# Starting the state-space layer of the first tile at once, and spreading the feed-forward weight quantisation over the first three passes

## Time and profile before

| | |
|---|---|
| median of three runs | 1433.84 us (1433.72 to 1434.61) |
| the profiled execution, its own time | 1433.73 us |
| its span, first to last instruction | 1431.3 us |
| instructions | 31673 |
| busy: PE, PE weight loads, DVE, ACT, POOL | 88%, 73%, 73%, 53%, 58% |
| mean granted TensorE clock | 0.98 |
| read and written in HBM | 19.74 MB, 4.19 MB |

### The profile page before, as it was taken

One profiled execution on the slowest core, in us unless ns is written; L12 is line 12 of the kernel. 1 busy time (PEld: TensorE's weight loads), 2 busy tenths in 40 slices (PEclk: granted clock), 3 DMA queues, 4 the chain that ended last, 5 costly groups with the idle time before them and its releaser, 6 DMA issues.

```text
span 1431.3 us, 31673 instructions
## 1 busy us (share of the span) xinstructions
PE 1266.4 (88%) x10486; PEld 1048.0 (73%) x10486; DVE 1043.3 (73%) x2485; ACT 755.8 (53%) x1740; POOL 827.7 (58%) x1404
## 2 busy tenths in 40 slices
PE   1478999999999999999999999999999999999874
PEld 0367887777787877777888777777887777878752
DVE  4546687777777777777877777778777777878655
ACT  1335455565555555655555556555555665555542
POOL 1425566565666665656666666566665666666541
PEclk9979999999999999999999999999999999999997
DMA  9100000000000000000000000000000000000000
GB/s 293 36 9 8 9 13 8 5 11 11 11 11 11 11 7 4 11 11 11 11 11 11 4 7 11 11 11 11 11 11 0 11 11 11 11 11 8 5 5 8
DMA packets 25361, 24.36 MB, mean 17 GB/s; under 512 B 6768, under 2 KB 23664, under 8 KB 25072
## 3 DMA queue, kind: packets, MB, share of 16 engines
q1 hardware_dynamic: 20848, 16.08, 3.7%
q10 hardware_dynamic: 4480, 7.86, 1.6%
HBM read 19.74 MB, written 4.19 MB: 17 GB/s over the span
## 4 chain that ended last, share of the span: by engine, by line
PE 47%; DVE 22%; POOL 14%; issue 9%; ACT 5%; SPq 1%; DMA 1%; DVEq 1%; POOLq 0%; ACTq 0%
PE bank L1344 15%; DVE xc L850 7%; POOL pr L440 5%; POOL pr L450 5%; PE bank L1336 5%; PE bank L1215 5%; PE bank L1149 3%; PE bank L1151 3%; PE bank L1150 3%; PE bank L1271 2%; PE bank L1166 2%; DVE h L997 2%; ACT h L683 2%; DVE h L1001 2%; PE bank L1324 2%
## 5 line engine op out<-in xcount | busy, mean ns | idle before, releaser
L1259 PE MATMUL bank<-xcT,wq 128*128 128x128 f32 x2048 | 238.5, 278 | 2.2 <-ACT xcT L629 2.2
L1259 PEld LDWEIGHTS bank<-xcT,wq 128*128 128x128 f32 x2048 | 233.3, 193 | 7.2 <-issue 2.0
L1344 PE MATMUL bank<-wo,oT 128*128 128x256 f32 x1024 | 231.3, 379 | 0.0
L1344 PEld LDWEIGHTS bank<-wo,oT 128*128 128x128 f32 x1024 | 191.8, 190 | 25.9
L850 DVE SCALAR_TENSOR_TENSOR xc<-bank,cw,xc 128x124 f32<-128x124 f32 (+2 forms) x576 | 163.8, 340 | 14.1 <-ACT xc L587 6.8
L450 POOL TENSOR_TENSOR pr<-pr,mx 128x512 f32<-128x512 f32 x64 | 78.9, 1254 | 90.5 <-DVE mx L963 90.5
L644 ACT ACTIVATE qT<-bank,bqT 128x128 f32<-128x128 f32 x384 | 108.4, 364 | 28.8 <-PE bank L1259 28.8
L652 ACT ACTIVATE q<-qT 128x512 f32<-128x512 f32 x128 | 81.4, 636 | 38.6 <-DVE qT L937 34.6
L997 DVE SCALAR_TENSOR_TENSOR h<-h,bank 128x512 f32<-128x512 f32 x64 | 44.0, 687 | 79.0 <-ACT h L683 79.0
L428 POOL TENSOR_TENSOR rq<-rq,minus_half 128x16 f32<-128x16 f32 x32 | 93.3, 2914 | 4.6 <-DVE rq L944 4.6
L1336 PE MATMUL bank<-pT,vb 64*128 64x256 f32 x512 | 72.9, 405 | 9.5 <-ACT pT L664 9.5
(11 more groups left out here) (233 smaller groups left out, 3273.6 us busy)
## 6 DMA issues: line engine op xcount, KB each, us to landing
x_in<-in_x SPq DMA_DIRECT2D x32, 128.0 KB, 2.0
c_in<-in_ctx SPq DMA_DIRECT2D x32, 128.0 KB, 2.0
out<-x SPq DMA_DIRECT2D x32, 128.0 KB, 1.7
wq<-in_L_xattn_Wq ACTq DMA_DIRECT2D x1, 2048.0 KB, 11.5
wo<-in_L_xattn_Wo ACTq DMA_DIRECT2D x1, 2048.0 KB, 19.3
w_in<-in_L_attn_W_in SPq DMA_DIRECT2D x1, 1288.0 KB, 11.7
qT<-in_L_ffn_w_gate ACTq DMA_DIRECT2D x1, 1024.0 KB, 6.7
q<-in_L_ffn_w_up SPq DMA_DIRECT2D x1, 1024.0 KB, 8.7
```

The source lines that it names most:

```text
L1259: last = mm(x_Qbank[g][:, (n % 4) * P:(n % 4 + 1) * P], wq[:, c, n * HD:(n + 1) * HD], xcT[:, c, :], start=(c == 0), stop=(c == DC - 1))
L1344: last = mm(X1[:, 0:D], oT[:, n, :, :], wo[:, n, :], start=(n == 0), stop=(n == NH - 1))
```

## The change: what it does

1. SP no longer issues w_up, and issues W_in (semaphore `w_in_l`) and W_out (`w_out_l`) after the twelve small weights. ACT issues w_gate, w_up and w_down as its first three instructions, w_down now into `oT`.
2. After its part of pass 0 (`body(0)`, which holds the load of x for tile 1), SP issues Wk (now into `pT`), Wv (now into `h_sq`), Wq, the two bias rows and Wo, which ACT issued before.
3. Pass -1 waits on PE for W_in alone; ACT makes `wz_hi` and POOL `wz_lo` ahead of it. W_out times norm_w, `wout_hi` and `wout_lo` come between pass -1 and pass 0, and PE waits for them before pass 0. `wk_hi`, `wv_hi`, `wk_lo`, `wv_lo` come between pass 0 and pass 1, and PE waits for them before pass 1.
4. The quantisation is cut into `w_sum`, `w_scale` and `w_round` on DVE, `w_total` and `w_turn` on PE and `w_turned` on ACT. They stand at chosen places inside passes -1, 0 and 1; w_gate is turned between pass 0 and 1, w_up and w_down between pass 1 and 2. Before pass 2 PE and DVE wait for all six copies. The totals use bank F0 in place of X0.
5. POOL computes the three constants `f_c` before pass 2 rather than before pass -1.

```diff
-        wk = q2[:, 0, :, :].rearrange("p h s -> p (h s)").rearrange("p (c n) -> p c n", c=DC)
-        wv = q2[:, 1, :, :].rearrange("p h s -> p (h s)").rearrange("p (c n) -> p c n", c=DC)
+        wk = pT[:].rearrange("p j n -> p (j n)").rearrange("p (c n) -> p c n", c=DC)
...
+        wv = h_sq[:].rearrange("p (c n) -> p c n", c=DC)
+        w_stage = [qT[:].rearrange("p a h s -> p (a h s)"), q2[:].rearrange("p a h s -> p (a h s)"),
+                   oT[:].rearrange("p h a s -> p (h a s)")]
+        w_tern = [hl[:].bitcast(BF16), h[:].bitcast(BF16), hl[:].bitcast(BF16)]
...
-            sp.dma_start(q2[:].rearrange("p a h s -> p (a h s)").rearrange("p (j n) -> p j n", n=D),
-                         w_up.rearrange("(j p) n -> p j n", p=P)).then_inc(s["w_up_l"].sem, 16)
-            sp.dma_start(w_in[:], W_in.rearrange("(c p) n -> p c n", p=P)).then_inc(s["w_mixer"].sem, 16)
...
-            sp.dma_start(w_out, W_out.rearrange("(j p) n -> p j n", p=P)).then_inc(s["w_mixer"].sem, 16)
+            sp.dma_start(w_in[:], W_in.rearrange("(c p) n -> p c n", p=P)).then_inc(s["w_in_l"].sem, 16)
+            sp.dma_start(w_out, W_out.rearrange("(j p) n -> p j n", p=P)).then_inc(s["w_out_l"].sem, 16)
             sp.dma_start(c_in[:], ctx_t[0]).then_inc(s["c_loaded"].sem, 16)
...
-            for i in range(5):
+            body(0)
+            sp.dma_start(wk, Wk.rearrange("(c p) n -> p c n", p=P)).then_inc(s["w_kv"].sem, 16)
+            sp.dma_start(wv, Wv.rearrange("(c p) n -> p c n", p=P)).then_inc(s["w_kv"].sem, 16)
+            sp.dma_start(wq[:], Wq.rearrange("(c p) n -> p c n", p=P)).then_inc(s["w_attn"].sem, 16)
+            sp.dma_start(bk_r[:], row(bk, NKV * HD)).then_inc(s["w_attn"].sem, 16)
+            sp.dma_start(bv_r[:], row(bv, NKV * HD)).then_inc(s["w_attn"].sem, 16)
+            sp.dma_start(wo[:], Wo.rearrange("(h p) n -> p h n", p=P)).then_inc(s["w_attn"].sem, 16)
+            for i in range(1, 5):
...
-            pool.wait_ge(s["w_mixer"].sem, 16 * W_MIXER)
-            g.tensor_tensor(w_out, w_out, bcast(nw[:, :].unsqueeze(2), [P, XCH, D]),
-                            ALU.mult).then_inc(s["p_wout"].sem, 1)
-            pool.wait_ge(s["p_hi"].sem, 2)
-            g.tensor_tensor(wz_lo[:], w_in[:, :, 0:DI], wz_hi[:].bitcast(F32), ALU.subtract).then_inc(s["p_lo"].sem, 1)
-            pool.wait_ge(s["p_wout"].sem, 1)
-            g.tensor_tensor(wout_lo[:], w_out, wout_hi[:].bitcast(F32), ALU.subtract).then_inc(s["p_lo"].sem, 1)
             pool.wait_ge(s["p_exp"].sem, 1)
             g.tensor_scalar(a_neg[:], a_neg[:], -1.0, None, ALU.mult).then_inc(s["p_scaled"].sem, 1)
-            pool.wait_ge(s["p_wout"].sem, 1)
...
+            pool.wait_ge(s["p_hi"].sem, 1)
+            g.tensor_tensor(wz_lo[:], w_in[:, :, 0:DI], wz_hi[:].bitcast(F32), ALU.subtract).then_inc(s["p_lo"].sem, 1)
+            body(*tiles(-1))
+            pool.wait_ge(s["w_out_l"].sem, 16)
+            g.tensor_tensor(w_out, w_out, bcast(nw[:, :].unsqueeze(2), [P, XCH, D]),
+                            ALU.mult).then_inc(s["p_wout"].sem, 1)
+            pool.wait_ge(s["p_hi"].sem, 2)
+            pool.wait_ge(s["p_wout"].sem, 1)
+            g.tensor_tensor(wout_lo[:], w_out, wout_hi[:].bitcast(F32), ALU.subtract).then_inc(s["p_lo"].sem, 1)
+            body(*tiles(0))
+            pool.wait_ge(s["p_hi"].sem, 3)
+            g.tensor_tensor(wk_lo[:], wk, wk_hi[:].bitcast(F32), ALU.subtract).then_inc(s["p_lo"].sem, 1)
+            pool.wait_ge(s["p_hi"].sem, 4)
+            g.tensor_tensor(wv_lo[:], wv, wv_hi[:].bitcast(F32), ALU.subtract).then_inc(s["p_lo"].sem, 1)
+            body(*tiles(1))
             pool.wait_ge(s["q_step"].sem, 9)
             g.tensor_scalar(f_c[:, 0:1], wmean[:, 0:1], 0.5 / QMAX, None, ALU.mult).then_inc(s["c_consts"].sem, 1)
             g.tensor_scalar(f_c[:, 1:2], wmean[:, 1:2], 1.0 / QMAX, None, ALU.mult).then_inc(s["c_consts"].sem, 1)
             g.tensor_scalar(f_c[:, 2:3], wmean[:, 2:3], 1.0 / QMAX, None, ALU.mult).then_inc(s["c_consts"].sem, 1)
             pool.wait_ge(s["c_consts"].sem, 4)
-            body(*tiles(-1))
-            pool.wait_ge(s["p_hi"].sem, 3)
-            g.tensor_tensor(wk_lo[:], wk, wk_hi[:].bitcast(F32), ALU.subtract).then_inc(s["p_lo"].sem, 1)
-            pool.wait_ge(s["p_hi"].sem, 4)
-            g.tensor_tensor(wv_lo[:], wv, wv_hi[:].bitcast(F32), ALU.subtract).then_inc(s["p_lo"].sem, 1)
-            for i in range(0, 5):
+            for i in range(2, 5):
...
-            act.dma_start(qT[:].rearrange("p a h s -> p (a h s)").rearrange("p (j n) -> p j n", n=D),
-                          w_gate.rearrange("(j p) n -> p j n", p=P)).then_inc(s["w_gate_l"].sem, 16)
+            for n, (w, cols) in enumerate(((w_gate, D), (w_up, D), (w_down, FF))):
+                act.dma_start(w_stage[n].rearrange("p (j n) -> p j n", n=cols), w.rearrange("(j p) n -> p j n", p=P)
+                              ).then_inc((s["w_gate_l"], s["w_up_l"], s["w_down_l"])[n].sem, 16)
+            def w_turned(n):
+                for half in range(2):
+                    act.wait_ge(s["q_t"].sem, 2 * n + half + 1)
+                    w = (wgT, wuT, wdT)[n][:].rearrange("p a b -> p (a b)")
+                    sc.copy(w[:, half * 1024:(half + 1) * 1024], (F0, F1)[half][:, :].bitcast(BF16)).then_inc(s["q_evac"].sem, 1)
...
-            act.wait_ge(s["q_bf"].sem, 1)
-            act.dma_start(qT[:].rearrange("p a h s -> p (a h s)").rearrange("p (j n) -> p j n", n=FF),
-                          w_down.rearrange("(j p) n -> p j n", p=P)).then_inc(s["w_down_l"].sem, 16)
-            act.dma_start(wq[:], Wq.rearrange("(c p) n -> p c n", p=P)).then_inc(s["w_attn"].sem, 16)
-            act.dma_start(wo[:], Wo.rearrange("(h p) n -> p h n", p=P)).then_inc(s["w_attn"].sem, 16)
-            act.dma_start(bk_r[:], bk.rearrange("(o n) -> o n", o=1).to_broadcast([P, NKV * HD])).then_inc(s["w_attn"].sem, 16)
-            act.dma_start(bv_r[:], bv.rearrange("(o n) -> o n", o=1).to_broadcast([P, NKV * HD])).then_inc(s["w_attn"].sem, 16)
...
-            for n in range(6):
-                act.wait_ge(s["q_t"].sem, n + 1)
-                if n == 1:
-                    act.wait_ge(s["q_bf"].sem, 2)
-                    act.dma_start(wk, Wk.rearrange("(c p) n -> p c n", p=P)).then_inc(s["w_kv"].sem, 16)
-                    act.dma_start(wv, Wv.rearrange("(c p) n -> p c n", p=P)).then_inc(s["w_kv"].sem, 16)
-                    act.wait_ge(s["p_wout"].sem, 1)
-                    sc.copy(wz_hi[:], w_in[:, :, 0:DI]).then_inc(s["p_hi"].sem, 1)
-                    sc.copy(wout_hi[:], w_out).then_inc(s["p_hi"].sem, 1)
-                w = (wgT, wuT, wdT)[n // 2][:].rearrange("p a b -> p (a b)")
-                sc.copy(w[:, (n % 2) * 1024:(n % 2 + 1) * 1024], (F0, F1)[n % 2][:, :].bitcast(BF16)).then_inc(s["q_evac"].sem, 1)
...
+            act.wait_ge(s["p_scaled"].sem, 3)
+            act.wait_ge(s["w_in_l"].sem, 16)
+            sc.copy(wz_hi[:], w_in[:, :, 0:DI]).then_inc(s["p_hi"].sem, 1)
             body(*tiles(-1))
+            act.wait_ge(s["p_wout"].sem, 1)
+            sc.copy(wout_hi[:], w_out).then_inc(s["p_hi"].sem, 1)
+            body(*tiles(0))
             act.wait_ge(s["w_kv"].sem, 32)
             sc.copy(wk_hi[:], wk).then_inc(s["p_hi"].sem, 1)
             sc.copy(wv_hi[:], wv).then_inc(s["p_hi"].sem, 1)
-            for i in range(0, 5):
+            w_turned(0)
+            act.wait_ge(s["q_bf"].sem, 2)
+            body(*tiles(1))
+            w_turned(1)
+            w_turned(2)
+            act.wait_ge(s["p_lo"].sem, 4)
+            act.wait_ge(s["q_bf"].sem, 3)
+            for i in range(2, 5):
...
+            def w_sum(n):
+                dve.wait_ge((s["w_gate_l"], s["w_up_l"], s["w_down_l"])[n].sem, 16)
+                v.tensor_reduce(wsum[:, n:n + 1], w_stage[n], AX.X, ALU.add, apply_absolute_value=True).then_inc(s["q_sum"].sem, 1)
+            def w_scale(n):
+                dve.wait_ge(s["q_tot"].sem, n + 1)
+                v.tensor_scalar(wmean[:, n:n + 1], F0[:, n:n + 1], 1.0 / (D * FF), QUANT_EPS,
+                                ALU.mult, ALU.max).then_inc(s["q_step"].sem, 1)
+                dve.wait_ge(s["q_step"].sem, 4 * n + 1)
+                v.reciprocal(winv[:, n:n + 1], wmean[:, n:n + 1]).then_inc(s["q_step"].sem, 1)
+                dve.wait_ge(s["q_step"].sem, 4 * n + 2)
+                v.tensor_scalar(w_stage[n], w_stage[n], winv[:, n:n + 1], 1.0, ALU.mult, ALU.min).then_inc(s["q_step"].sem, 1)
+            def w_round(n):
+                dve.wait_ge(s["q_step"].sem, 4 * n + 3)
+                v.tensor_scalar(w_stage[n], w_stage[n], -1.0, ROUND, ALU.max, ALU.add).then_inc(s["q_step"].sem, 1)
+                dve.wait_ge(s["q_step"].sem, 4 * n + 4)
+                if n == 2:
+                    dve.wait_ge(s["q_t"].sem, 2)
+                v.tensor_scalar(w_tern[n], w_stage[n], ROUND, None, ALU.subtract).then_inc(s["q_bf"].sem, 1)
...
```

(87 more changed lines are left out.)

21 lines of the change are left out of this document (4 added, 17 removed).

## The result

The changed kernel took 1439.74 us (median of 8 runs, 1436.88 to 1442.27), the kernel before 1434.38 beside it: a ratio of 1.0035, 95% interval 1.0024 to 1.0046. The forecast was 1429.5, faster, with a range up to 1436.0. It was wrong in sign and by 10 us. The profiled execution took 1441.29 with a span of 1438.7, 7.4 more than before.

The account below looks back on a forecast made before the run. PE with its chain's waits sets the rhythm, so only pass 2's earlier start counts: 22.5 - 6.5 - 1.5 - 4.9 - 4.4 - 1.0 = 4.2 us gained, from 1433.73 to 1429.5; range 1423.5 to 1436.

Parts of the forecast that it names:

- The head: Pass -1: POOL's `1/sqrt` at 25.8 instead of 48.34, a lead over the old kernel of 22.5 us.
- T: Time W_in is in the core, in the head: taken as 22.2 us, between 17.5 and 30.1.
- Between pass -1 and pass 0: Splitting W_out makes PE wait before pass 0: 8.5 us lost, 2.0 regained, so 6.5 off the lead.
- DVE pays 1.8 us and POOL nothing: Side by side with POOL's `wout_lo`, a DVE step took 3.05 instead of 1.28; POOL would not be slowed.
- taken back: Before pass 0: 2.0 us regained because `wk_lo` and `wv_lo` no longer delay pass 0's segment sums; bounds 0 and 4.7.
- The DVE steps inside pass 0: Summing, scaling and rounding placed in DVE's waits in pass 0: 1.5 us lost, at `w_round(1)`; bounds 0 and 3.3.
- between pass 0 and 1: `wk_lo` and `wv_lo` delay POOL's `x_norm` by 4.7 us, PE 0.2 more: 4.9 lost; SP's transfers arrive in time.
- Between pass 1 and 2: ACT's copies of turned weights delay PE's scores: 4.5 us lost, 0.1 returned, so 4.4; bounds 4.0 and 6.0.
- the clock: Half clock after PE's near-idle stretches before passes 1 and 2: 1.0 us charged, bounds 0 and 4.2.
- The loop: Everything behind the start of pass 2 was to move along with it, in settled passes of 37.4 us; no loss charged.
- The stalls cost what the head gives: Rival: half clock falls fully on passes 1 and 2, 3.2 us more than charged, 1432.7, no change; chance 0.19.
- a late W_in: Rival in the head: W_in lands at 30.1, lead gone from 26.4 on, time 1437.4, slower; chance 0.11.

Follow-up runs that it names:

- Experiment 11: Kernel with late splitting and late turning, plus W_in issued right after x_in and small weights behind, awaited only at dt: 1406.33 us, ratio 0.9812 to the kernel before.
- experiment 4: Changed kernel with the splitting of W_out, Wk and Wv moved from between the passes into them, waits at first use: 1420.95 us, ratio 0.9918 to the kernel before.
- experiment 15: Changed kernel with one more wait on DVE ahead of pass 2 (395 instructions ahead of the loop): 1436.01 us, ratio 1.0018 to the kernel before.
- experiment 14: Changed kernel with one more instruction on POOL near its start, DVE left at 394: 1436.97 us, ratio 1.0027 to the kernel before.
- experiment 7: Changed kernel with two more instructions on DVE near its start (396 ahead of the loop): 1434.70 us, ratio 1.0008 to the kernel before.
- experiment 8: Changed kernel with four more instructions on DVE near its start (398 ahead of the loop): 1434.52 us, ratio 1.0009 to the kernel before.
- experiment 5: Changed kernel with one redundant wait on DVE near its start (395 ahead of the loop): 1434.01 us, ratio 1.0005 to the kernel before.
- experiment 16: Changed kernel with eight more instructions on DVE near its start (402 ahead of the loop): 1433.37 us, ratio 1.0005 to the kernel before.
- Experiment 3: Changed kernel with products that nothing reads on PE in its three long waits before passes 0, 1 and 2: 1436.89 us, ratio 1.0030 to the kernel before.
- experiment 6: Kernel before the change with one redundant wait on DVE near its start (394 ahead of the loop): 1438.48 us, ratio 1.0031 to the kernel before.

## Why the prediction was wrong

**The head: right, but T partly by luck.** T = 22.2 was measured as 22.96, `m_mv` at 25.8 as 26.62, the lead of 22.5 as 21.7. The small weights did stand in the way: they kept W_in's issue back to 15.66, and the transfer then took 7.3. The prediction had reached its T from bytes and a 4.7 us stall; its other estimate had the issue at 18.4 and the transfer at 11.7, both too long. Experiment 11 shows that the next 11 us lay in the head.

**Between pass -1 and pass 0: the step that failed first.** The forecast took 6.5; by L910 12.4 were gone. Three things, each a sentence of the prediction. "DVE pays 1.8 us and POOL nothing": POOL paid 2.9, because each of its small steps ended only when DVE's long one did (37.14 + 1.13 = 38.27 beside 36.92 + 1.29 = 38.21, and so twice more). The old trace had shown it in one direction only because a POOL step had started first there. The Trainium skill had it (Advanced Engine Details and Errata, VectorE Performance Modes), and its page SBUF — State Buffer (Who interferes with whom) says more closely that whichever starts first holds the shared pair of ports for its whole instruction. The trace agrees: the three blocked POOL steps ended 0.05 to 0.07 after DVE's. Then "the x projection takes 2.05 in the head at whatever clock": that row stood behind 8 us in which PE had worked with no wait above 1.4, as the old trace shows and the prediction did not look up; behind 12.17 of waiting it took 3.78. That the wait made it slow is argued and not shown: in experiment 4 it took 3.79 behind 8 us of work with no wait above 0.79 (PE had stood still for the 27.9 us before them). And of the 2.0 "taken back" at most 0.9 came: the lead fell from 21.7 to 10.2 by the first x projection, 11.5 for the 8.5 of the prediction and POOL's 2.9, and by 0.8 more to L910, with the projection itself 1.7 longer. The segment sums' input waited behind `wout_lo` and not behind `wk_lo` and `wv_lo`.

**The DVE steps inside pass 0, and between pass 0 and 1: right.** 1.5 was 1.3, 4.9 was 4.3. Experiment 4 adds what the forecast did not ask: these waits were of the change's own making. SP's transfers were in time, as said: Wo landed at 65.2, pass 1 started at 84.5.

**Between pass 1 and 2, and the clock: mis-sized.** 4.4 was 3.9. For the clock 1.0 was charged; the x projection of pass 1 (1.7) and the scores of pass 2 (1.3) alone make 3.0. Together the lead fell by 6.9 from `x_mv` to the first x2 where 5.4 were charged.

The profiles show more of the clock than these two rows. Eight of them are of kernels that do the same work: the changed one, twice, and it with idle waits added. Here are the mean granted clock from 50 to 130 us and the start of the first x2:

| kernel | clock | first x2 |
|---|---|---|
| changed, first and second profile | 0.72, 0.74 | 163.21, 162.32 |
| experiments 15, 14 | 0.72, 0.74 | 163.72, 162.02 |
| experiments 7, 8 | 0.77, 0.79 | 160.05, 159.85 |
| experiments 5, 16 | 0.81, 0.81 | 157.74, 157.47 |

The more of that stretch ran at 1.2 and not at 2.4 GHz, the later came the first x2, by up to 6 us. The kernel before had 0.81, and 160.05. Against it the clock took the 3.0 of above; but by the two rows with 0.81, an estimate from them, the changed kernel would have led by some 2.4 at the first x2 with its clock, and it was 3.2 behind with 0.72. So differences of up to 5.6 went with the clock, which was charged with 1.0 and bounded by 4.2. Experiment 3, where PE had work in its waits, had 0.86 and its first x2 at 156.05, which supports the clock as the cause; its median (1436.89) does not show the gain. Between the two profiles of the changed kernel itself 0.9 went with it. Whether the waits near the start (experiments 5, 7, 8, 16) brought the better clock, or chance did, no run tells: there is one profile of each.

**The loop: put at nothing.** By the prediction "everything behind it moves along". It did not: 0.95 was lost in the first loop pass and 0.13 on average in each of the 25 later ones, 4.1 in all; in the second profile of the same kernel 0.95 and 0.05, 2.3 in all. Here is the first loop pass of the changed kernel, on ACT, DVE, POOL and PE, with two rows of the second pass:

```profile
261.52 0.60 ACT L627 ACTIVATE decay<-bank 128x512 f32<-128x512 f32 x1
...
303.58 0.60 ACT L627 ACTIVATE decay<-bank 128x512 f32<-128x512 f32 x1
```
```profile
262.59 0.68 DVE L895 TENSOR_TENSOR mbd<-decay,gm 64x512 f32<-64x512 f32 x1 [2.42 <-ACT decay L627]
...
264.34 1.13 DVE L828 TENSOR_SCALAR m_xn<-x_in,m_mv 128x256 f32<-128x256 f32 x1
...
304.40 0.69 DVE L895 TENSOR_TENSOR mbd<-decay,gm 64x512 f32<-64x512 f32 x1 [2.17 <-ACT decay L627]
```
```profile
264.17 1.15 POOL L403 TENSOR_TENSOR yy<-xs,d_par 128x512 f32<-128x512 f32 x1 [1.88 <-ACT xs L633]
```
```profile
265.53 0.44 PE L1190 MATMUL bank<-ident,m_xn 128*128 128x128 f32 x2 [0.99 <-DVE m_xn L828]
```

and of experiment 15, which differs by one wait:

```profile
262.05 0.60 ACT L627 ACTIVATE decay<-bank 128x512 f32<-128x512 f32 x1
...
303.08 0.60 ACT L627 ACTIVATE decay<-bank 128x512 f32<-128x512 f32 x1
```
```profile
262.76 0.68 DVE L895 TENSOR_TENSOR mbd<-decay,gm 64x512 f32<-64x512 f32 x1 [2.05 <-ACT decay L627]
...
264.50 0.41 DVE L828 TENSOR_SCALAR m_xn<-x_in,m_mv 128x256 f32<-128x256 f32 x1
...
303.78 0.68 DVE L895 TENSOR_TENSOR mbd<-decay,gm 64x512 f32<-64x512 f32 x1 [2.05 <-ACT decay L627]
```
```profile
264.70 1.71 POOL L403 TENSOR_TENSOR yy<-xs,d_par 128x512 f32<-128x512 f32 x1 [1.88 <-ACT xs L633]
```

ACT's decay ends at 262.12 and DVE answers 0.47 later; in experiment 15 at 262.65 and DVE answers after 0.11. DVE is 0.36 late with nothing to wait for that the trace shows. POOL's `yy` then starts ahead of `m_xn` and not behind it, holds the shared ports, and `m_xn`, which PE waits for, takes 1.13 and not 0.41; PE loses 0.99. In the fast order of experiment 15 POOL pays instead (1.71), where it costs nothing; in nine of the twelve profiles with another count than 394 neither pays (`yy` 1.10 or 1.11, `m_xn` 0.41).

The lateness does not end with the first pass. It sits at one DVE step, the one that answers ACT's decay (L895), and in all six profiles with 394: 0.47 or 0.48 in the first loop pass, 0.20 to 0.22 in each of the 25 later ones, and 0.10 or 0.11 again in the first pass behind the loop. In all twelve others the same step answers after 0.10 to 0.12 in every pass from pass 1 on. So it belongs to the loop's code at that place and not to how the engines enter the loop. `m_xn` took 1.13 in the first loop pass of all six and 0.41 in all twelve. That a count of 394 makes DVE late there is shown; why is not. That it has to do with how DVE gets its instructions at that point would fit, and no run here tells. All the added instructions stand ahead of the loop, so the count ahead of it and the length of DVE's whole program changed together.

**The sum, redone.** In the two profiles the forecast had a gain of 4.2 and the trace shows a loss of 7.3 at the last x2. The 11.5 between them are 0.8 (head), 5.9 (between pass -1 and 0), -0.2 (DVE steps), -0.6 (between pass 0 and 1), -0.5 (between pass 1 and 2), 2.0 (clock behind `x_mv`) and 4.1 (loop). The largest is the second.

In the times the terms are less sure. By the ratios the change costs 5.0 to 5.4 us. At the fast places (experiments 5, 7, 8, 15, 16) the ratio is 1.0009 in the mean, so 1.3 us, and the loop's place would be 4. But in four of these five the first x2 was earlier too, by 2.3 to 5.7, with a better clock. Experiment 15, where it was not, gives 1.0018, so 2.4 to 2.9 for the place; the kernel before lost 4.4 by it (experiment 6). With DVE out of POOL's way as well the ratio is 0.9985: by that the port is 3.4, by the profile 1.9 at the first x2. The slow x projections are no term that I can show in the times. What remains between -2.2 and the forecast's -4.3, 2 us, I leave open; it is less than what the first x2 moves among seven kernels that differ in waits alone (157.5 to 163.7), and these follow the clock as in the table above.

**The rivals.** "The stalls cost what the head gives" (0.19) had one of the right mechanisms, the half clock, and gave 1432.7: it lacked the port and the loop. The one for slower, a late W_in (0.11), came nearest in time with 1437.4, and that was luck: W_in landed at 22.96, where the rival had 30.1 and needed more than 26.4. A version that beats both kernels is that of experiment 11: 1406.33, 1.9% under the kernel before.

## What to carry to other kernels

Work that must be done before some product should be waited for at that product and not at the head of the pass: that was worth 18.7 us here by the medians, 15.5 of it seen at the first `x_mv`, and the wait was the change's own. Before forecasting less than half a per cent for a kernel with a loop, measure the kernel with one idle instruction more on its busy engines; here one on DVE alone moved either kernel by some 5 us. Compare the granted clock of the two profiles in the same stretch before a difference of a few us is put down to the change. And when a long DVE step is put into a wait, look at what POOL does in that wait.

## What the runs showed of the hardware that was not expected

- One redundant wait on DVE changed the loop's first pass from 42.05 to 41.01 us, in a place-dependent way: 394 instructions ahead are slow, 393, 395, 396, 398 and 402 are not. With 394 one DVE step answers its semaphore 0.21 after the release in each loop pass (0.47 in the first), with the others 0.11.
- A long DVE step and a POOL step side by side, in the rows shown here: the later one ends with the earlier one or after it. DVE steps of 1.29 and 1.23 took 2.50 and 3.25, POOL steps of 0.20 took 1.13 to 1.19, one of 2.34 took 3.39.
- After a wait of 5.91 us PE's projection took 3.78, after one of 3.22 it took 2.05; but in experiment 4 it took 3.79 after one of 0.79, so the last wait alone does not decide. The granted clock in the record was 1.00 in the stretches in which the first slow projections ran (45 to 50) and 0.50 from 60 to 70, so the record of the first 50 us does not show the slowness that the durations show.
- The drain behind the last loop pass (x2 of tile 28 to that of tile 31) took 97.2 to 97.7 us in nine executions and 99.2 to 99.7 in nine, and the changed kernel had both. The mean granted clock over it was 0.965 in each of the nine shorter and 0.93 to 0.95 in the nine longer.
